# GpSimd's scatters of the experts' rows, issued one after another: each waits for the landing of the one in front of it

## What is computed

```python
# layer 0
x = x + ga * softmax_attention(h)              # 16 heads of 16
h = layernorm(x) * (1 + cb) + sb
x = x + gb * moe0(h)                           # 16 experts, 2 per token, 256 rows an expert and batch; more are dropped
# layer 1
x = x + ga * linear_attention(h)               # causal
h = layernorm(x) * (1 + cb) + sb
attn = softmax(q k^T) v                        # 16 heads
moe  = sum over the 2 best of 8 experts: g * (h @ W_experts[e] + b_experts[e])
x = x + gb * (attn + moe)
```

## Time and profile before

| | us |
|---|---|
| median of 3 runs (lowest, highest) | 3529.8 (3527.66, 3538.92) |
| span of the profiled execution, first to last instruction | 3643.8 |
| busy in the span: PE, DVE, ACT, GpSimd | 3409.9, 3033.2, 2545.1, 515.1 |
| mean granted TensorE clock | 0.954 of full speed |

### The profile page before, as it was taken

The page is one execution under the profiler, slowest core; times in us unless marked ns, Lnnn a source line. Parts: engine busy times, 40 slices in busy tenths (PEclk is TensorE's granted clock), DMA queues, the critical chain, the costliest instruction groups (busy, mean ns, idle before and its releaser), DMA issues. The chain is left out here.

```text
span 3643.8 us, 74382 instructions
## 1 busy us (share of the span) xinstructions
PE 3409.9 (94%) x29746; PEld 1567.3 (43%) x29746; DVE 3033.2 (83%) x3971; ACT 2545.1 (70%) x4700; POOL 515.1 (14%) x405
## 2 busy tenths in 40 slices
PE   9999999999999998757889875999999999999998
PEld 5433333333333333646667644733333333333333
DVE  8899999999999993623676644299999999999993
ACT  3188888888888887323223322588888888888887
POOL 4410000000000000341321133034430010000001
PEclk9699999999999999878999987999999999999999
DMA  9552020202202001334100475523120212202001
GB/s 260 125 162 39 14 42 16 38 18 40 38 14 43 14 10 30 134 129 139 32 26 12 119 191 164 166 56 61 44 58 16 38 52 52 38 15 43 14 16 46
DMA packets 307729, 233.29 MB, mean 64 GB/s; under 512 B 206359, under 2 KB 258488, under 8 KB 302738
## 3 DMA queue, kind: packets, MB, share of 16 engines
q1 hardware_dynamic: 291076, 179.46, 21.8%
q0 software_dynamic: 14832, 47.79, 4.0%
q10 hardware_dynamic: 1504, 1.64, 0.1%
HBM read 126.49 MB, written 102.76 MB: 63 GB/s over the span
## 5 line engine op out<-in xcount | busy, mean ns | idle before, releaser
L907 ACT ACTIVATE att_l_probs<-att_l_s_ps 128x512 f32<-128x512 f32 x4096 | 2214.1, 595 | 312.2 <-PE att_l_s_ps L837 247.1
L926 DVE TENSOR_REDUCE att_in_part_max<-att_l_max_ps 128x2 f32<-128x1024 f32 x1952 | 2328.4, 1218 | 12.2 <-PE att_l_max_ps L825 11.1
L852 PE MATMUL att_l_o_ps<-att_l_probs,att_l_v_sb 128*17 128x256 f32 x16384 | 1271.3, 385 | 1.1 <-ACT att_l_probs L907 1.1
L837 PE MATMUL att_l_s_ps<-att_in_q_sb,att_in_k_sb 50*128 50x512 f32 x2048 | 758.3, 446 | 9.0 <-DVE att_l_o_ps L943 9.0
L837 PE MATMUL att_l_s_ps<-att_in_q_sb,att_l_k_sb 50*128 50x512 f32 x2048 | 743.0, 448 | 1.1 <-ACT att_l_probs L907 0.9
L825 PE MATMUL att_l_max_ps<-att_l_k_sb,att_in_q_sb 50*128 50x512 f32 x2048 | 724.9, 444 | 0.8 <-DVE att_in_part_max L926 0.7
L825 PE MATMUL att_l_max_ps<-att_in_k_sb,att_in_q_sb 50*128 50x512 f32 x1856 | 664.6, 448 | 0.3 <-DVE att_in_part_max L926 0.3
L852 PEld LDWEIGHTS att_l_o_ps<-att_l_probs,att_l_v_sb 128*17 128x17 f32 x16384 | 278.3, 95 | 720.6 <-issue 383.5
L837 PEld LDWEIGHTS att_l_s_ps<-att_in_q_sb,att_in_k_sb 50*128 50x128 f32 x2048 | 311.6, 185 | 443.6 <-ACT att_l_probs L907 408.6
L837 PEld LDWEIGHTS att_l_s_ps<-att_in_q_sb,att_l_k_sb 50*128 50x128 f32 x2048 | 308.1, 184 | 437.1 <-ACT att_l_probs L907 395.0
L825 PEld LDWEIGHTS att_l_max_ps<-att_l_k_sb,att_in_q_sb 50*128 50x128 f32 x2048 | 291.0, 184 | 7.7 <-DVE att_in_part_max L926 7.3
(11 more groups left out here) (262 smaller groups left out, 2870.1 us busy)
## 6 DMA issues: line engine op xcount, KB each, us to landing
att_in_q_sb<-q_hi SPq DMA_DIRECT2D x256, 64.0 KB
slot_rows<-att_l_zeros POOLq DMA_DIRECT2D x10, 1024.0 KB
ffn_parts<-slot_rows SPq DMA_DIRECT2D x40, 256.0 KB
tile_out<-ffn_parts SPq DMA_DIRECT2D x40, 256.0 KB, 2.1
att_in_q_sb<-q_lo SPq DMA_DIRECT2D x128, 72.0 KB
att_l_v_sb<-v_rows SPq DMA_DIRECT2D x16, 544.0 KB, 14.2
att_in_k_sb<-k_hi SPq DMA_DIRECT2D x32, 256.0 KB, 9.6
att_l_k_sb<-k_hi SPq DMA_DIRECT2D x32, 256.0 KB
```

The lines of the kernel that those rows point to most:

```text
L837: nc.tensor.matmul(s_ps[:, c % SB], k_sb[j // GPB % 2][rows, pair, u * P:(u + 1) * P], q_sb[rows, j % QR, pair], start=True, stop=True).th ...
L852: last = nc.tensor.matmul(o_ps[32 * h:32 * h + AUG, cols], v_sb[:, j // GPB % 2, u, h * AUG:(h + 1) * AUG], probs[:, u % 2, h, cols], star ...
L907: nc.scalar.activation(probs[:, u % 2, h], s_ps[:, c % SB], ACT.Exp, scale=float(HD) ** -0.5).then_inc(exp_done, 1)
L926: nc.vector.reduce_max(part_max[:, j % 2, k], max_ps[:, r], AX.X).then_inc(slot_taken, 1)
```

## The change

Ahead of every scatter but a batch's first, GpSimd waits until all scatters of that batch issued so far have landed (16 on the semaphore for each). Nothing else is changed: the same 128 scatters, in the same order, with the same data. A batch's first scatter doesn't wait for the batch before it.

```diff
             def put(b, s0, s1):
-                for k, t in [divmod(s, TPB) for s in range(s0, s1)]:
+                for s in range(s0, s1):
+                    k, t = divmod(s, TPB)
+                    if s > 0:
+                        pool.wait_ge(rows_put[b], 16 * s)
                     nc.gpsimd.indirect_dma_start(
                         out=io.slot_rows, out_offset=bass.IndirectOffsetOnAxis(ap=put_at[:, b, k, t:t + 1], axis=0),
                         in_=m.z_all[:, b * TPB + t], in_offset=None,
@@
                 for k in range(2):
                     for t in range(TPB):
+                        s = k * TPB + t
+                        if s > 0:
+                            pool.wait_ge(rows_put[b], 16 * s)
                         nc.gpsimd.indirect_dma_start(
                             out=io.slot_rows, out_offset=bass.IndirectOffsetOnAxis(ap=m.get_at[:, b, k, t:t + 1], axis=0),
```

## The result

The changed kernel takes 3746.7 us (median of 4 runs, 3740.33 to 3751.23); the kernel before, run beside it, takes 3528.7 us (4 runs). The ratio is 1.062, 95% interval 1.060 to 1.064: 218 us slower. The forecast was 164 us slower and a range that ended at 3740, so the direction held and the size did not. The profiled execution of the changed kernel took 3740.33 us, 1.7 us more than its span.

A forecast was written before the change was run, and what follows sets the result against it. The ends of the two layers' experts' parts, each followed by a barrier, were taken to bound the kernel. 87 (layer 0) + 67 (layer 1) + 10 (clock) = 164 on 3529.8 gave 3694 us, range 3590 to 3740.

The forecast's parts named there:

- The base: Experts' parts of both layers: 120 us of delays in the shown trace, 59 and 61, are absent from timed runs.
- the first rival: Experts' parts of both layers: timed runs have the delays, the serialized chain takes their place; +34, 3564 us; chance 0.12.
- the pitch: Distance between starts of successive scatters in both layers: 2.95 us with the waits, between 2.40 and 3.08, from 1.28.
- layer 1's base: Layer 1 without delays or waits: item 39's transposes at 2291.4 in place of 2352.1, 61 us earlier.
- Layer 0, +87 forecast: 64 scatters in one chain land at 1685.2, 18 items follow: end at 1743.9 against 1656.5.
- Layer 1, +67 forecast: 64 scatters in one chain land at 2307.1: item 39's transposes at 2358.1 against 2291.4.
- The clock, +10: PE restarts at the lower clock after the waits before items 16 and 20, 5 us each.
- Not hidden: Answers the rival that waits are met at once or covered by slack in the items: 3530 us, chance 0.04.
- Spacing that pays: Rival: real delays vanish with one scatter in flight; faster below 2.68 us a scatter, 3494 us at 2.40; chance 0.05.
- the signs that the forecast named: Profile after: scatters 2.95 us apart, SP's loads near 1685 and 2307, PE idle some 50 us, span 3650 to 3700.

The follow-up runs named there:

- clean trace: Kernel before, no edit, profiled again to see whether the stalls of the shown trace recur: 3529.5 us, ratio 1.0005, profiled span 3536.4 us.
- the run alone: Waits between scatters only in layer 1, none in layer 0, against the kernel before: 3643.2 us, ratio 1.033, +117.
- second set: On one chip: all waits 3748.7 us, every fourth scatter waiting 3561.6, every eighth 3534.7, the kernel before 3528.3 (3533.4 in its profiled run).
- two in flight: Each scatter waits for the one before the last, two semaphores a batch, against the kernel before: 3563.8 us, ratio 1.010, +37.

## Why the prediction was right in direction and wrong in size

**The base: right, for a reason that was half right.** The stalls taken out of the shown trace (120 us) are not in the timed runs: a clean trace has a span of 3536.4. But "the delays belong to the profiled execution alone" was too narrow. They belong to a kind of chip; two of those used later are slower by as much in every run, and their traces show the stalls in the stages that were left unchanged. That the shown profile came from such a chip is inferred from its stalls and its span; its chip isn't known. Each of the four chips of the experiments was used for one set of runs only, so whether it is the chip or its condition in that hour isn't shown either. On the two slower chips the first rival, real delays beside a longer chain, happens: 3784 against 3654. What the prediction weighed at 0.12 is true there, with +130 where it had +34.

**The failed step: the pitch.** "I take 2.95", between 2.40 and 3.08, "and some 3.3 where other transfers are in the way". Measured: 3.17 to 3.21 in quiet stretches, so landing (2.4) and issue (0.8) add up without any overlap, and the 0.1 us that I saved for a reaction counted twice is not there. The mean of layer 0 is 3.30. Under the stores of layer 1 it is not 3.3 but 7.8. That bound was the worst of it: it named the place, and no row stood behind its 3.3. The second term that failed is layer 1's base, 21.6 us too short, and it hides part of this, as told below. The page "DMA: Bandwidth & Descriptors" of the Trainium skill, in "Anatomy of one DMA — SWDGE (gpsimd) path", gives by estimate 2.3 us for these bytes. The trace agrees for a lone scatter (2.4), and the 7.0 us beside 95% busy engines show that it is no price for a crowded one.

**Layer 0, +87 forecast, about +107 measured** (267.8 us from first scatter to end of the items, against 160.3). The chain landed 210.3 us behind its first start (1707.0 − 1496.7) and not 188.8: +21. Behind the landing all went as worked out: 57.5 us for the 18 items, where 58.7 stood. (The base of 1656.5 was right too: the clean trace has 160.3 us against its 160.2, although its terms add up to 1656.4.)

**Layer 1, +67 forecast, about +108 in the traces, +117 by the run alone.** From the first scatter to item 39's transposes:

| us from the first scatter | forecast | measured |
|---|---|---|
| before | 173.1 | 194.7 (2043.54 to 2238.23) |
| after: last landing | 188.8 | 246.8 (to SP's load at 2390.96) |
| after: item 39 | 239.8 | 302.6 (to 2446.70) |

The base was 21.6 us short, since SP's first load stands behind its loads of queries and keys until 2109.47, 65.9 us behind the first scatter. The chain was 58 us longer: 39 of it in the first eight steps (62.6 against 8 x 2.95), the other 19 in 55 steps that are a quarter of a microsecond longer than forecast, a few of them beside the item loads longer still. The short base makes the loss too large and the short chain makes it too small; together with the clock's 4.7 us below they leave 41 us. That the forecast of this layer was no further off is luck.

**The clock, +10.** Layer 0 shows one group of eight matmuls at 3.56 us and the next at 1.89 (1710.88, 1715.57), 1.7 us; behind the last landing PE was still no later than worked out without it. Layer 1 is 4.7 us later than worked out (55.7 from the load to item 39, against 51.0). So about 5, already contained in the 107 and 108.

**Sum.** 87 + 67 + 10 = 164; with the terms as measured 107 + 108 = 215, and the timed medians differ by 218. The two spans differ by only 202.2: the stretch ahead of the first scatter is 1.7 us shorter after, the one from layer 0's items to layer 1's first scatter 5.2, the attention behind layer 1's experts 6.3. The 5.2 us go with the clock, a gain that the forecast didn't have: in that stretch the granted clock is 0.96 after and 0.95 before (in its first 100 us 0.93 and 0.88), and the same 3010 matmuls (3011 recorded after) keep PE busy for 342.1 and 347.5 us. The second set's pair, from one chip, has the same, 341.9 and 347.4. For the 6.3 us the windows show less: a granted clock of 0.97 and 0.96 in the first 400 us, by estimate 4 us. That 215 comes so near to 218 is partly luck, since it sets parts of single executions against medians: the profiled execution of after was the quickest of its four, that of before among the slower of its eight.

**The other rivals.** Not hidden: PE idles 61 us in layer 0 and 80 us in layer 1 ahead of its items. Spacing that pays: not with a wait at every scatter on either kind of chip, but with one at every fourth on the second kind, 0.987. Its mechanism, stalls that vanish with the trains, was the right one; the pitch that it needed, 2.68 or less, is reached only by spacing less.

Of the signs that the forecast named, the idle time in front of each scatter and PE's stand at item 16 came as told. SP's loads of items 16 and 20 came at 1707.0 and 2391.0, not near 1685 and 2307, and the span, 3738.6, lies above the 3650 to 3700.

No version beat the kernel before on the first kind of chip. On the second, every fourth did, by 50 us, in four runs on one chip; every eighth was not tried there.

## What to carry to other kernels

A wait for each DMA's landing costs the whole latency plus the issue at every step, so price it as their sum (3.2 us here), and price each stretch by the load on the DMA engines there: 2.4 us to land when they are free, 7.0 when other transfers keep them 95% busy. The loss is not the number of waits but how far they move a landing that somebody already waits for. In layer 0, where the last landing had no slack, two in flight moved it and the stage's end by 21 and 22 us; in layer 1 the last scatter moved by 47 us and the items' end by 19. In time, two in flight gave back 181 of 218 us, a wait at every eighth 212. Where a profile's span and the timed runs differ by several per cent (here 3.2), find out on which chip each was taken before pricing anything that stands near the stalls.

## What the runs showed of the hardware that was not expected

On two of the chips the kernel before takes 3651.5 to 3663.4 us in 14 of 14 runs, and on the others 3518 to 3543 us in all. The traces taken on these two chips, all of kernels with some waits, show, in stages that are as in the kernel before, stalls of PE, ACT and DVE for each other's results, up to 16 us each on PE, while GpSimd sends indirect DMAs back to back every 1.3 us. They are absent while each scatter waits for the last landing, or every fourth does, and they return some 9 us into a train of gathers. Why some chips show this and others don't, whether it stays with a chip from one hour to the next, and which resource it is, no run here tells. Also unexpected was that a scatter's landing nearly triples, from 2.4 to 7.0 us, beside another queue's transfers: q1, SP's, takes 88.4% of the DMA engines' time in that stretch and GpSimd's own q0 6.2%.
